# One load for each third of the step rates: reshaping the partition spread of a selective-scan kernel and giving each slot a semaphore of its own

## What is computed

```
xz = x @ in_proj_w.T;  xc, z = split(xz)             # 192 channels each
xa = silu(depthwise_conv3x3(xc) + conv_b)
xs = [xa by rows, xa by columns, both of them flipped]           # K = 4 directions, L = 4096
dts, Bs, Cs = x_proj_w[k] @ xs[k]                    # 6, 16 and 16 rows
delta = softplus(dt_proj_w[k] @ dts + dt_proj_b[k])  # 192 channels
for l in range(L):                                   # for each direction, channel d and state n
    h = exp(delta[l] * A) * h + (delta[l] * xs[l]) * Bs[l]
    y[l] = sum_n(h * Cs[l]) + xs[l] * D
```

## Time and profile before

| | |
|---|---|
| median of three runs | 12636.41 us (12634.88 to 12658.96) |
| time of the profiled execution | 12636.41 us |
| its span, first to last instruction | 12634.5 us |
| VectorE busy, first to last product of the scan phase (10057.5 us) | 9240.8 us |
| GpSimd busy in the same stretch | 9011.4 us |
| ScalarE busy in the same stretch | 7057.7 us |
| mean busy share of the 16 DMA engines in the same stretch | 0.51 |
| loads that fill `dur` and `dlr` | 2048 of 384 KB |

### The profile page before, as it was taken

The page is one execution under the profiler, slowest core; times in us unless marked ns, Lnnn a source line. Parts: engine busy times, 40 slices in busy tenths (PEclk is TensorE's granted clock), DMA queues, the critical chain, the costliest instruction groups (busy, mean ns, idle before and its releaser), DMA issues. The chain is left out here.

```text
span 12634.5 us, 236253 instructions
## 1 busy us (share of the span) xinstructions
PE 10880.0 (86%) x91896; PEld 5769.9 (46%) x91896; DVE 10716.4 (85%) x6806; ACT 8121.0 (64%) x13314; POOL 9743.6 (77%) x4238
## 2 busy tenths in 40 slices
PE   8888888888888888888888888888888888699999
PEld 5633433443333343433333434333334343577878
DVE  7789989998999999989999999899999998455554
ACT  3367767776777667767776677677766776344443
POOL 2179888988898889888988898889888988433330
PEclk9978888888888888888888888888888888799999
DMA  3344554455455545554455455545554554231220
GB/s 106 109 109 112 121 129 111 114 121 129 111 116 122 129 110 118 122 126 112 114 122 128 111 115 122 126 113 116 122 128 111 115 122 96 72 73 49 61 61 11
DMA packets 380191, 1363.70 MB, mean 108 GB/s; under 512 B 55270, under 2 KB 55974, under 8 KB 375756
## 3 DMA queue, kind: packets, MB, share of 16 engines
q1 hardware_dynamic: 379084, 1348.57, 45.5%
HBM read 983.45 MB, written 364.90 MB: 107 GB/s over the span
## 5 line engine op out<-in xcount | busy, mean ns | idle before, releaser
L909 POOL TENSOR_TENSOR HC<-H,crep 128x1024 f32<-128x1024 f32 x3072 | 7210.5, 2376 | 1051.4 <-DVE H L737 1050.7
L737 DVE TENSOR_TENSOR_SCAN H<-E,car,psum 128x1024 f32<-128x1024 f32 x1920 | 4473.0, 2343 | 488.1 <-PE psum L640 424.3
L598 PE MATMUL psum<-sx,selb 96*128 96x512 f32 x4864 | 2160.2, 537 | 1206.2 <-DVE H L737 898.7
L821 ACT ACTIVATE E<-dlr,am 128x1024 f32<-128x1024 f32 x2560 | 2916.7, 1143 | 247.8 <-DVE H L737 243.8
L662 PE MATMUL psum<-HC,sely 128*32 128x512 f32 x12288 | 2684.7, 737 | 150.7 <-POOL HC L909 150.7
L598 PEld LDWEIGHTS psum<-sx,selb 96*128 96x128 f32 x4864 | 912.6, 232 | 2996.8 <-DVE H L737 1768.3
L715 DVE TENSOR_TENSOR psum<-dur,psum 128x1024 f32<-128x1024 f32 x1792 | 2165.9, 1209 | 59.1 <-PE psum L598 59.1
L640 PEld LDWEIGHTS psum<-diag,dluT 128*32 128x32 f32 x49152 | 1411.0, 116 | 812.1 <-issue 402.5
L640 PE MATMUL psum<-diag,dluT 128*32 128x128 f32 x49152 | 1640.2, 290 | 162.1 <-DVE H L737 161.5
L737 DVE TENSOR_TENSOR_SCAN H<-E,psum 128x1024 f32<-128x1024 f32 x640 | 1453.8, 2283 | 184.2 <-PE psum L640 153.5
L827 ACT COPY car<-H 128x1 f32<-128x1 f32 x2304 | 422.3, 183 | 1638.6 <-DVE H L737 1638.6
(11 more groups left out here) (135 smaller groups left out, 11281.5 us busy)
## 6 DMA issues: line engine op xcount, KB each, us to landing
dur<-scr_dlu SPq DMA_DIRECT2D x1024, 384.0 KB, 6.7
dlr<-scr_dl SPq DMA_DIRECT2D x1024, 384.0 KB, 10.1
scr_dl<-dlt SPq DMA_DIRECT2D x256, 384.0 KB, 6.5
scr_dlu<-dlu SPq DMA_DIRECT2D x256, 384.0 KB, 3.2
scr_yk<-yt SPq DMA_DIRECT2D x256, 384.0 KB, 13.4
yp<-scr_yk SPq DMA_DIRECT2D x128, 384.0 KB, 5.7
scr_xa<-xs SPq DMA_DIRECT2D x64, 384.0 KB, 3.5
scr_sz<-xs SPq DMA_DIRECT2D x64, 384.0 KB, 3.3
```

The source lines that it names most:

```text
L598: r = e.matmul(o[:, sub * 512:(sub + 1) * 512], selb[:, which, :], sx[:, c % 2, sub * 512:(sub + 1) * 512], start=True, stop=True)
L737: e.tensor_tensor_scan(H[:, un % NH, ::step], decay[:, ::step], drive[:, ::step], init, ALU.mult, ALU.add).then_inc(scan_done)
L821: e.activation(o, dlr[:, slot(m, j), :], ACT.Exp, scale=am[:, ae:ae + 1]).then_inc(exp_done)
L909: e.tensor_tensor(HC[:, un % NHC, :], H[:, un % NH, :], crep[:, g, :], ALU.mult).then_inc(hc_done)
```

## The change

The four loads of a step (one for each copy, 32 partitions, three thirds together) become three loads (one for each third `j`, all 128 partitions, four copies together). The source of a load is 32 rows of the scratch tensor, repeated four times by a broadcast dimension with step zero that stands ahead of the rows: `[4, 32, TC]`. The destination is one slot: 128 partitions x 1024 values. Each of the six slots of `dlr` and of `dur` gets its own semaphore, so there are 12 where there were 4. Readers wait for the slot of their unit (16 for each load) and no longer for all loads of the step. A load of third `j` waits only for the last reader of that third in step m - 2, in the order j = 0, 1, 2; the wait for GpSimd's products keeps its count. `out_dl` and `out_dlu` wait for three semaphores where they waited for one.

```diff
-    dlr_in = [sem(f"dlr_in{i}") for i in range(2)]
-    dur_in = [sem(f"dur_in{i}") for i in range(2)]
+    dlr_in = [sem(f"dlr_in{i}") for i in range(2 * NJ)]
+    dur_in = [sem(f"dur_in{i}") for i in range(2 * NJ)]
...
     def loaded(m):
-        return 64 * (m // 2 + 1)
+        return 16 * (m // 2 + 1)
...
         def out_dl(m):
             if m >= 2:
-                e.wait_ge(dlr_in[m % 2], loaded(m - 2))
+                for j in range(NJ):
+                    e.wait_ge(dlr_in[slot(m, j)], loaded(m - 2))
...
-        def spread_rows(t, name, m, landed):
-            for q in range(4):
-                e.dma_start(t[32 * q:32 * q + 32, NJ * (m % 2):NJ * (m % 2) + NJ, :],
-                            S[name][m % 2].rearrange("(j d) t -> d j t", j=NJ)).then_inc(landed[m % 2], 16)
-
         def in_dur(m):
             e.wait_ge(dlu_out, 16 * (m + 1))
-            if m >= 2:
-                e.wait_ge(mul_done, muls(last_of(m - 2, kinds=(DIRECT,))) + 1)
-                e.wait_ge(pool_mul_done, pooled(12 * (m - 1)))
-            spread_rows(dur, "dlu", m, dur_in)
+            for j in range(NJ):
+                if m >= 2:
+                    e.wait_ge(mul_done, muls(last_of(m - 2, j=j, kinds=(DIRECT,))) + 1)
+                    e.wait_ge(pool_mul_done, pooled(12 * (m - 1)))
+                e.dma_start(dur[:, slot(m, j), :],
+                            S["dlu"][m % 2, 32 * j:32 * j + 32, :].unsqueeze(0).to_broadcast([4, 32, TC])).then_inc(
+                                dur_in[slot(m, j)], 16)
 
         def in_dlr(m):
             e.wait_ge(dl_out, 16 * (m + 1))
-            if m >= 2:
-                e.wait_ge(exp_done, 12 * (m - 1))
-            spread_rows(dlr, "dl", m, dlr_in)
+            for j in range(NJ):
+                if m >= 2:
+                    e.wait_ge(exp_done, last_of(m - 2, j=j) + 1)
+                e.dma_start(dlr[:, slot(m, j), :],
+                            S["dl"][m % 2, 32 * j:32 * j + 32, :].unsqueeze(0).to_broadcast([4, 32, TC])).then_inc(
+                                dlr_in[slot(m, j)], 16)
...
-            e.wait_ge(dur_in[m % 2], loaded(m))
+            e.wait_ge(dur_in[slot(m, j)], loaded(m))
             e.tensor_tensor(P[un % 2], dur[:, slot(m, j), :], P[un % 2], ALU.mult).then_inc(mul_done)
...
-            e.wait_ge(dlr_in[m % 2], loaded(m))
+            e.wait_ge(dlr_in[slot(m, j)], loaded(m))
```

More of the change, by code:

```diff
@@ L501, in out_dlu @@
             if m >= 2:
-                e.wait_ge(dur_in[m % 2], loaded(m - 2))
+                for j in range(NJ):
+                    e.wait_ge(dur_in[slot(m, j)], loaded(m - 2))
             e.wait_ge(dlu_made, m + 1)
             e.dma_start(S["dlu"][m % 2], dlu[:]).then_inc(dlu_out, 16)
-        def spread_rows(t, name, m, landed):
-            for q in range(4):
-                e.dma_start(t[32 * q:32 * q + 32, NJ * (m % 2):NJ * (m % 2) + NJ, :],
-                            S[name][m % 2].rearrange("(j d) t -> d j t", j=NJ)).then_inc(landed[m % 2], 16)
         def in_dur(m):
             e.wait_ge(dlu_out, 16 * (m + 1))
-            if m >= 2:
-                e.wait_ge(mul_done, muls(last_of(m - 2, kinds=(DIRECT,))) + 1)
-                e.wait_ge(pool_mul_done, pooled(12 * (m - 1)))
-            spread_rows(dur, "dlu", m, dur_in)
+            for j in range(NJ):
[5 more added lines that the diff above has]
+                                dur_in[slot(m, j)], 16)
         def in_dlr(m):
             e.wait_ge(dl_out, 16 * (m + 1))
-            if m >= 2:
-                e.wait_ge(exp_done, 12 * (m - 1))
-            spread_rows(dlr, "dl", m, dlr_in)
+            for j in range(NJ):
+                if m >= 2:
[3 more added lines that the diff above has]
+                                dlr_in[slot(m, j)], 16)
         def store_y(m):
```

## The result

| | before | after |
|---|---|---|
| median | 12635.65 us (4 runs) | 13048.74 us (13031.66 to 13064.05, 4 runs) |
| ratio | | 1.0324, 95% interval 1.0305 to 1.0344 |
| profiled execution's time and span | 12636.41 and 12634.5 us | 13056.9 and 13055.0 us |

The direction and the range of rival A (12,640 to 13,100 us, chance 0.22) held; the forecast of 19,600 us didn't.

A forecast was written before the change was run, and what follows sets the result against it. VectorE's scans and products, with GpSimd beside, bound it now; four-stream loads would make chained transfers 132.4 us a pair against 78.6, adding 6,890 us plus 105 for `u` to 12636.4: 19,600 us; 8-in-10 range 12,640 to 21,000 us.

The forecast's parts named there:

- rival A: Loads on four streams at the fast rate, 65.3 us a pair, costing only by late landing: 12,640 to 13,100 us, chance 0.22.
- Nothing waits for the loads now, so finer waits are worth 0 us: Waits of readers and ahead of loads: no compute engine waits for `dur` or `dlr`, so meeting waits sooner gains 0 us.
- Three issues for four, 0 us: SyncE's queue: one load issue of 0.45 us less, some 0.9 us a step on a waiting queue, worth 0 us.
- Four streams: Loads of `dur` and `dlr`: four copies outermost in the source leave four streams, twelve of sixteen DMA engines getting nothing.
- I take 13.3 GB/s a stream: Loads of `dur` and `dlr`: each stream carries a sixteenth of 212 GB/s, so 6.29 MB take 118.7 us a pair.
- The nearest rows are those of `dur` and `dlr` themselves: Reason for the slow rate: today's loads read the same source rows four times into the same buffers at 212 GB/s.
- all the time: Reason for the slow rate: four streams walking 32 neighbouring partitions at the same pace always stand 32 partitions apart.
- The chained sum: Transfers of a pair of steps in sequence: 118.7 + 7.1 + 6.6 = 132.4 us, against 78.6 us now.
- loads + 7.1 + 6.6 us: Per pair: the loads, 7.1 us of other transfers on the busy engines, 6.6 us of round trips waiting for stores.

## Why the prediction went wrong, point by point

- *Nothing waits for the loads now, so finer waits are worth 0 us*: right for loads that come in time, 12,641 us with the waits alone. With the loads on four streams they give back 372 us, a term that stood at nothing in rival A as well. *Three issues for four, 0 us*: the prediction took 0.45 us for each, and three took 14.0. No run parts what that blocking costs from what the slower loads cost.
- *Four streams*: right. A DMA share of 0.25 in the loads' windows, 0.13 with two copies, and the loss gone with the rows outermost. The rule of the Trainium skill, "DMA: Bandwidth & Descriptors", "Why a DMA increments its semaphore by 16 and not by 1", agrees in all of these cases, and with a share of 0.51 for eight copies.
- *"I take 13.3 GB/s a stream"*: this is the step that failed. The term stood at 118.7 us a pair. Measured are 100 to 105 GB/s in place of 53, so 6.29 MB take 61 us. I had two reasons. "The nearest rows are those of `dur` and `dlr` themselves" was a wrong choice of nearest: those rows show what sixteen streams get together into 32 partitions, 213 GB/s, and sixteen streams into 128 partitions got 281 to 406 GB/s. A sixteenth of a rate that sixteen streams share is not what one of them can carry; two and four had 25.8 GB/s each. The second reason, streams that stand 32 partitions apart "all the time", held for some microseconds only: 35 to 37 GB/s, then 49 to 53 for two of them. For eight streams, with 15 to 16 GB/s each, it may hold nearly all the time; that is not shown.
- The port rule of the Trainium skill ("SBUF — State Buffer", "Door 1: The DMA port swizzle") fits the slow 32-partition loads (213 GB/s), the faster 128-partition ones (281 to 406) and the slow start 32 apart (35 to 37). What it doesn't say is whether streams keep in step, and that was the point here. Why two and four streams get faster after their start no run shows.
- *The chained sum* (loads + 7.1 + 6.6 us): right in form. With the rate of the changed kernel's windows put in, it foretold 20,000 us for two streams, and 20,011 were measured. With the right rate the changed kernel has 61 + 6.7 + 6.6 = 74 us of transfers in a pair of 78.6 us: the chain doesn't bound.
- *Rival A* then describes what happened: loads that decide only by landing late, "0 to 3.5 us a pair". Measured: 3.3 us. But in the step that it followed it had ScalarE held for 6 us and VectorE for nothing or 1 us, through the decay of the last third alone. In the trace VectorE pays in three places: behind late decays (58 us named, 133 us under "issue"), for `dur` itself (158 us), and for fills of TensorE, which stands behind ScalarE's late copies (87 us more). The kernel without the finer waits lies outside A's range, at 13,421 us: that the change landed inside it is owed to them, and A had them at 0.
- *The chances* gave the failed rate 0.50 and A 0.22, though by its own words nothing but the step between streams spoke for the slow one. It also took the 385 GB/s of the earlier trace rows for the rate of transfers that meet each row of HBM once, and didn't weigh the load of `u` in the earlier trace rows, which meets each row once too and is slower (184 GB/s at a share of 0.77).

## What to carry to other kernels

Put a dimension that sixteen engines can share evenly (32, 96 or 128 entries here) outermost on both sides of a DMA; a broadcast of four copies in front of it leaves twelve engines idle, and it shows at once as a share of 0.25 in windows where only loads run. (With the rows outermost the copies of a row lie side by side, so the rest of the kernel has to be laid out for that; the runs here only timed it.) Before taking a rate from the "nearest" transfer, ask what limits that transfer (streams, partitions reached, or source), because a limit of the old shape needn't exist in the new one, and measure the new rate instead of scaling one by the number of streams: a stream had 25.8 GB/s with two or four running, and 15 to 16 with eight. A transfer that fits by throughput can still cost by landing late: 74 us of transfers in a 78.6 us pair cost 3.3 us, while half of the loads' bytes cost nothing. Finer waits were worth 372 us with late loads and nothing with punctual ones.

## What the runs showed of the hardware that I hadn't expected

- The issue of a load blocks SyncE when few streams have much queued. Three `dlr` loads took 14.0 us to issue on four streams and 2.2 us on sixteen; the longest single issue was 12.4 us on four streams, and with two streams the median was 8.5 us. From the tile view of `dlr`, the issues' ns min/median/max; the changed kernel:

```profile
L523 SPq DMA_DIRECT2D dlr<-scr_dl x768: 499/532/12383, 646.9 to 11092.0; - x192
```

  sixteen streams:

```profile
L523 SPq DMA_DIRECT2D dlr<-scr_dl x768: 512/553/1757, 647.6 to 10665.4; - x192
```

  two streams:

```profile
L523 SPq DMA_DIRECT2D dlr<-scr_dl x768: 486/8456/17823, 655.6 to 18034.8; - x192
```

- Two streams that write partitions 32 apart get 35 to 37 GB/s together for some microseconds and then 49 to 53; 64 apart they have 49 to 53 GB/s nearly from the start.
- Eight streams of 16 partitions each carry about 123 GB/s most of the time, little more than four streams of 32 partitions (100 to 105).
- A load over 128 partitions on sixteen streams runs at 281 to 406 GB/s, where loads over 32 partitions from the same rows run at 205 to 225 GB/s.
